# Linear attention's opening on one core: rows loaded in pieces, the first experts' chunk handled a slot later, the third tile's moments earlier, and ranks counted with float16 ones

## What is computed

```python
# block 0: linear attention over a context
q = query @ Wq.T
gate = sigmoid(query @ Wg.T + bg)
k, v = split(kv @ Wkv.T)
q, k = feature_map(q), feature_map(k)      # x + 1 where x > 0, else exp(x)
kv_summary = einsum('bhsd,bhse->bhde', k, v)
z = 1.0 / (einsum('bhld,bhd->bhl', q, k.sum(-2)) + EPS)
out = einsum('bhld,bhde->bhle', q, kv_summary) * z
out = out * gate @ Wo.T
# block 1: 8 experts, the two best per token, and a shared one
ew, ei = top_k(x @ gate_w.T, 2)
```

## Time and profile before

| what | value |
|---|---|
| three runs | 391.04, 392.04 and 392.64 us, median 392.04 |
| the profiled execution | 392.65 us, its span 390.8 us |
| busy in the span | PE 372.2, DVE 292.0, ACT 244.2, POOL 224.6 us |
| transfers | 38.14 MB, 98 GB/s on average |
| the chain that ended last | PE 57%, POOL 16%, DVE 14%, issue 7%, DMA 2% |

### The profile page before, as it was taken

One profiled execution on the slowest core, in us unless ns is written; L12 is line 12 of the kernel. 1 busy time (PEld: TensorE's weight loads), 2 busy tenths in 40 slices (PEclk: granted clock), 3 DMA queues, 4 the chain that ended last, 5 costly groups with the idle time before them and its releaser, 6 DMA issues.

```text
span 390.8 us, 10015 instructions
## 1 busy us (share of the span) xinstructions
PE 372.2 (95%) x3258; PEld 330.4 (85%) x3258; DVE 292.0 (75%) x836; ACT 244.2 (62%) x563; POOL 224.6 (57%) x376
## 2 busy tenths in 40 slices
PE   8799999998999999999999999899999989999996
PEld 7588888887878888998999999677777779999996
DVE  5689988998988879754544499877889895775533
ACT  4666776565545442467866887767777778634550
POOL 4455567478886774603441678688887876541100
PEclk9899999999999999999999999999999999999999
DMA  7661221132322256458784532111120000010111
GB/s 245 204 189 46 74 75 48 37 106 67 97 97 88 83 187 190 130 159 272 232 275 152 176 96 68 56 55 55 55 57 3 2 3 2 2 55 29 44 40 55
DMA packets 31188, 38.14 MB, mean 98 GB/s; under 512 B 4385, under 2 KB 28322, under 8 KB 31138
## 3 DMA queue, kind: packets, MB, share of 16 engines
q1 hardware_dynamic: 28066, 29.11, 24.4%
q0 software_dynamic: 3072, 8.39, 6.4%
HBM read 24.90 MB, written 12.58 MB: 96 GB/s over the span
## 4 chain that ended last, share of the span: by engine, by line
PE 57%; POOL 16%; DVE 14%; issue 7%; DMA 2%; ACT 1%; SPq 1%; POOLq 0%; ACTq 0%; DVEq 0%
PE PS L334 10%; PE PS L336 9%; PE PS L335 9%; PE PS L2262 8%; PE PS L2280 8%; POOL xs_rows L710 3%; POOL rj L769 2%; POOL rows_early L753 2%; PE PS L2097 2%; PE PS L2000 2%; POOL wfl L482 2%; POOL sj L773 1%; SPq L516 1%; PE PS L1920 1%; DMA arena_f<-xs_rows 1%
## 5 line engine op out<-in xcount | busy, mean ns | idle before, releaser
L1101 ACT ACTIVATE arena_f<-PS,cols 128x256 f16<-128x256 f32 x64 | 26.5, 472 | 21.6 <-PE PS L2262 19.1
L334 PE MATMUL PS<-wfh,arena_r 128*128 x117 | 35.1, 300 | 1.8 <-DVE arena_r L1601 1.0
L334 PE MATMUL PS<-w0h,arena_r 128*128 128x256 f32 (+1 forms) x96 | 34.7, 362 | 0.3 <-POOL arena_r L434 0.2
L335 PE MATMUL PS<-wfl,arena_r 128*128 x117 | 33.0, 282 | 0.0
L336 PE MATMUL PS<-wfh,arena_r 128*128 x117 | 32.8, 281 | 0.0
L2262 PE MATMUL PS<-arena_r,w1h 128*128 128x256 f32 x128 | 31.2, 284 | 0.0
L335 PE MATMUL PS<-w0l,arena_r 128*128 128x256 f32 (+1 forms) x96 | 31.1, 324 | 0.0
L336 PE MATMUL PS<-w0h,arena_r 128*128 128x256 f32 (+1 forms) x96 | 31.1, 324 | 0.0
L2262 PE MATMUL PS<-arena_r,w1l 128*128 128x256 f32 x128 | 31.0, 283 | 0.0
L488 POOL TENSOR_TENSOR w1l<-raw,w1h 128x384 fp32r<-128x384 f32 (+1 forms) x14 | 12.7, 914 | 30.7 <-ACT w1h L474 30.6
L710 POOL DMA_INDIRECT xs_rows<-rows_early,posi x24 | 24.2, 1010 | 8.9 <-issue 6.7
(11 more groups left out here) (316 smaller groups left out, 1388.5 us busy)
## 6 DMA issues: line engine op xcount, KB each, us to landing
arena_f<-xs_rows SPq DMA_DIRECT2D x39, 128.0 KB, 2.5
ys_rows<-raw SPq DMA_DIRECT2D x19, 256.0 KB, 2.7
raw<-in_w_ffn SPq DMA_DIRECT2D x16, 241.0 KB, 2.6
raw<-in_w_l SPq DMA_DIRECT2D x12, 192.0 KB, 2.7
ctx_raw<-in_ctxT SPq DMA_DIRECT2D x16, 128.0 KB, 2.2
out<-arena_f SPq DMA_DIRECT2D x7, 256.0 KB, 2.1
raw<-in_w_l SPq DMA_DIRECT2D x5, 256.0 KB, 4.7
x<-in_x SPq DMA_DIRECT2D x1, 1280.0 KB, 6.3
```

The costliest lines, as they stand in the source:

```text
L334: nc.tensor.matmul(out_ap, lh, rh, start=first, stop=False)
L335: nc.tensor.matmul(out_ap, lh, rl, start=False, stop=False)
L1101: nc.scalar.activation(md16[:, g % 2, n, :], PS[:, M_H[n // 2], (n % 2) * D:(n % 2 + 1) * D], ACT.Gelu, bias=cols[:, 2 * KC + n:2 * KC + n ...
```

## The change

Five things are done. **SP:** x's tiles 2 and 3 are issued between the second and the third piece of block 0's weights, with a semaphore of their own; the transfer of tiles 6 to 15 becomes three, of tiles 6 and 7, 8 to 11 and 12 to 15, the latter two behind the context tiles 4 and 5 and the experts' chunks 2 and 3, for which the first round of SP's loop is written out. **DVE:** in slot 0 the moments of tiles 2 and 3 come before the split of the fourth piece of weights and the bias. **ACT:** in slot 0 the norm of tile 2 comes before `split_hi(4)`. **ACT and POOL:** the experts' chunk 0 is split in slot 1, just ahead of chunk 1, and not at the end of slot 0. **Ranks:** `member`, `below` and the ones of three of the rank matmuls become float16 (with one more copy on DVE in slot 4); the matmul that adds the carry and the one for the totals stay float32.

```diff
-        below, ones = sb("below", [P, P]), sb("ones", [P, P])
+        below, ones16, ones = sb("below", [P, P], F16), sb("ones16", [P, P], F16), sb("ones", [P, P])
-        member = raw[:, 2020:2148].rearrange("p (t e) -> p t e", e=EXPERTS)
+        member = raw[:, 2020:2084].bitcast(F16).rearrange("p (t e) -> p t e", e=EXPERTS)
...
             for i in range(4):
                 load(raw[:, W0_AT[i]:W0_AT[i + 1]], A["w_l0"][:, W0_AT[i]:W0_AT[i + 1]], w0_in[i])
+                if i == 1:
+                    load(x[:, 2:4, :], x_d[:, 2:4, :], x_in[1])
             load(bg_raw[:, :], A["bg"], const_in)
-            load(x[:, 2:4, :], x_d[:, 2:4, :], const_in)
...
             load_w(0, 0, 0)
-            load(x[:, 6:TILES, :], x_d[:, 6:TILES, :], x_in[1])
+            load(x[:, 6:8, :], x_d[:, 6:8, :], w0_in[4])
             load_w(0, 1, 1)
...
-            with sp.Fori(1, TILES // 2 - 1) as i:
+            for r, (a, b) in enumerate(((8, 12), (12, TILES))):
+                load_ctx(4 + r, r)
+                load_w(0, 2 + r, r)
+                load(x[:, a:b, :], x_d[:, a:b, :], x_in[1 - r])
+
+            with sp.Fori(2, TILES // 2 - 1) as i:
...
(POOL, slot0)
-                if tile := s.tile(0):
+                if s.is_at(1):
+                    weights_lo_step(pool, 0, 0, 0)
+                if (tile := s.tile(0)) and s.at:
                     weights_lo_step(pool, 0, *tile)
...
(ACT, slot0)
                 if s.is_at(0):
+                    norm(2)
                     split_hi(4)
...
                 if s.is_at(0):
                     ctx_hi_step(act, 2, 0)
-                    norm(2)
...
-                if tile := s.tile(0):
+                if s.is_at(1):
+                    weights_hi_step(act, 0, 0, 0)
+                if (tile := s.tile(0)) and s.at:
                     weights_hi_step(act, 0, *tile)
...
(DVE)
                     nc.vector.tensor_scalar(below[:, :], step[:, :], lane[:, 0:1], None, ALU.is_gt)
+                    nc.vector.tensor_copy(ones16[:, :], ones[:, :])
...
             split_w0(2)
-            split_w0(3)
-            dve.wait_ge(const_in, 16 * 3)
-            bias_parts(bg_raw[:, :], 2)
+            dve.wait_ge(x_in[1], 16)
             for t in range(2, 4):
                 moments(t)
+            split_w0(3)
+            dve.wait_ge(const_in, 16 * 2)
+            bias_parts(bg_raw[:, :], 2)
...
                 if s.is_at(2):
-                    dve.wait_ge(x_in[1], 16)
+                    dve.wait_ge(w0_in[4], 16 * 3)
+                if s.is_at(4):
+                    dve.wait_ge(x_in[1], 16 * 2)
+                if s.is_at(8):
+                    dve.wait_ge(x_in[0], 16 * 3)
...
(PE, rank_members)
                     last = nc.tensor.matmul(
-                        rank[:, t + 1:, :], ones[:, :],
+                        rank[:, t + 1:, :], ones16[:, :],
```

## The result

The changed kernel takes **393.04 us** (median of 22 runs, 391.62 to 396.22) against 391.87 us of the kernel before (22 runs beside it, 390.52 to 393.08): ratio **1.0035**, 95% interval 1.0022 to 1.0047. It is slower by 1.2 us, where 390.2 us, a gain of 1.8, was forecast.

The account below looks back on a forecast made before the run. Bound in the opening by the POOL-to-ACT chain to tile 2's norm, with PE's stall and the lowered clock behind it. Opening 1.8, less 0.6 for context tile 4, plus 0.6 for ranks: 1.8 us gain, 390.2 us, range 388.8 to 392.2.

Parts of the forecast that it names:

- Slot 0 and 1: Opening: norm of tile 2 1.5 us earlier, gate product at 12.75, attention of tile 0 1.4 us earlier and 0.4 shorter.
- Every sign that was listed as right: Norm near 13.4 us, gate product a us later, attention near 17.0, full clock, context tile 4 awaited, 4 float16 rank rows per batch.
- those listed as wrong: Slot 4 of PE no earlier, ACT waiting over 1.5 us for chunk 2, clock below full in slots 1-3, POOL's stretch without idling before.
- Opening gain so far: 1.8 us: Slots 0 and 1: attention 1.4 us earlier plus 0.4 us less time at full clock; between 1.0 and 2.2 us.
- the opening loses twice: Opening, 9.8 to 19.5 us: time lost by PE's 1.66 us stall and by the lowered clock behind it.
- Chunk 0, priced at 0: Experts' chunk 0 split in slot 1: chunk 2 up to 1.5 us late at no cost, covered by ACT's idling in slot 3.
- Context tile 4, "gives back 0.6 us": Slots 2 and 3: tile issued at 21.1, lands about 1.1 us late, giving back 0.6 us, between 0 and 0.9.
- The slack of 0.45 us: Behind context tile 4: about 0.15 us on ACT and DVE, 0.3 between the gated rows and their transposes.
- Ranks, 0.6 us: Last rank batch: float16 matmuls take 0.2 us instead of 0.8, a gain of 0.6, or 0.4 at float32 spacing.
- The step that put the last batch on the chain: Ranks: of the four batches only the last is on the chain, so its 0.6 us counts in the sum.
- D: Rival, slower: chunk 2 lands after 27 us on SP's one queue, ACT and PE stall in slots 2 and 3; 394.8 us, chance 0.07.
- C: Rival: gain lost to slower transfers of x's pieces and chunk 1, or a later stage; 391.5 to 392 us, chance 0.11.

Follow-up runs that it names:

- e18: The kernel before with float16 ranks and four overwritten float16 matmuls of 32 columns ahead of each batch's, PE's program at 3258 instructions as before: ratio 0.9997.
- e2: The kernel before with only the ranks' ones, comparison mask and membership in float16: ratio 1.0040 to the kernel before.
- e5: The kernel before with only the float16 ranks, run once more for a second trace and more times: ratio 1.0060 to the kernel before.
- e17: The kernel before, float32 ranks, with two overwritten float32 matmuls of 8 columns ahead of each batch's, PE's program 16 instructions longer (3274): ratio 1.0067.

## Why the prediction was wrong, by its steps

- **Slot 0 and 1**: right. Norm at 13.06 (13.35 said), gate product at 12.34 behind the bias (12.75), attention at 16.71 (17.0) in 0.69 us, no fall of the clock in the trace. Every sign that was listed as right came, and none of those listed as wrong: the signs looked at the opening, and the loss lies behind it.
- **"Opening gain so far: 1.8 us"**: right against one trace, and that was the failure of its base. The step that reads the earlier trace rows as a property of the kernel, "the opening loses twice", held in 57 of 96 executions. In the others the clock doesn't fall, and where a trace shows such an execution the stall is there. Against one of those the opening was ahead by 1.3 us and not 2.1, before context tile 4 took 1.0 of it. Of the 1.2 us that the opening with its give-back fell short, about 0.3 come from this base (39 of 96 times the 0.7 us between the two groups) and 0.4 to 0.6 from context tile 4, below; what is left is about as large as the interval. The text had even put the profiled execution 0.6 us above the median, and took it as a shift of the whole rather than as part of what was to be won.
- **Chunk 0, priced at 0**: the number was right for itself (pieces alone 1.0005), but what it is worth beside the earlier norm, up to 1.8 us, was missed. Chunk 2 landed at 26.46 and cost ACT 0.51 us of waiting, as bounded.
- **Context tile 4, "gives back 0.6 us"**: the mechanism was right, the size was off. Issued at 20.09 and not 21.1, awaited 1.27 us and not 1.1, it took 1.0 to 1.2 us of PE's lead, above the bound of 0.9. The slack of 0.45 us on the way was not there. Issuing it first wins that back (0.9997 to 0.9966).
- **Ranks, 0.6 us**: the step that failed most. The local gain is 0.69 us, a little over the upper gain of 0.6; what it brings at the end is 0 (`e18`), because once PE comes sooner the scatters on POOL set when the experts' rows are there. The step that put the last batch on the chain and carried its whole gain to the end is what was wrong.
- **What no step had**: float16 ranks with PE's program 16 instructions shorter cost 1.2 to 2.3 us by medians (`e2`, `e5`), where the sum had a gain of 0.6, and nothing with the 16 put back. By what path the number of instructions acts stays open. No rival ended there. D, the only slower one, was a stall on SP's queue; it didn't happen. C, "a later stage takes the gain back", has the right outcome for the opening but not by its mechanism.

## What to carry to other kernels

A stall with a fall of the clock behind it in one profile may be a stall alone in the next execution: look at the granted clock of many executions before the fall is counted as gain. When an edit changes the number of instructions on an engine, test it once more with neutral instructions that restore the number; here that separated nothing from 1.2 to 2.3 us. But the neutral instructions have a time of their own, which must be read too. And an edit that frees one path is to be tried with its companions taken away one by one: the earlier norm was a loss without the later chunk and the cut rows, and worth nothing with them until the next transfer in line was moved as well.

## What was not expected of the hardware

- With 3242, 3266 or 3274 instructions on PE instead of 3258, kernels take 0.2 to 0.7% more than their like, whichever type the instructions added or removed have. Up to 0.8 us of it in `e17` is the added matmuls' own time. One disturbed chip doesn't show it. The matmul at 214.33 us of the changed kernel starts 0.1 us late with no wait shown, in all five undisturbed traces with 3242 instructions and in none with 3258. Whether other lengths are good again was not tried.
- A mean clock of 0.991 or less is in none of the 96 executions of before, but in 1 of 12 and 2 of 10 of the ranks alone, 1 of 22 of the changed kernel and 2 of 6 of `e17`. No kept trace of these kernels has one.
- The kernel before has two lengths, 389.8 and 390.5 us of span, as the clock falls or doesn't behind the same 1.67 us of idling.
- One chip ran every kernel 10 us slower than the others, with 3.6 us of waiting on DVE and 6.2 on ACT put down to something outside the core's engines; what that is stays open.
- The wait for one expert's weights varies: ACT waited 3.06 us for it in the trace of the opening alone, 1.61 in that of before, 0.78 in that of the pieces alone, and it cost PE 1.7 us in the first.

```profile
181.98 0.52 ACT L474 ACTIVATE w1h<-raw 128x384 fp32r<-128x384 f32 x1 [3.06 <-DMA raw<-in_w_l]
```
